# Moving the scaling, rounding and turning of attention's output rows into the next batch's attention

## The reference, cut to what matters

```
def _qdq(x):
    s = jnp.maximum(jnp.max(jnp.abs(x), axis=-1, keepdims=True) / 127.0, 1e-08)
    return jnp.clip(jnp.round(x / s), -127.0, 127.0) * s
...
attn = jax.nn.softmax(jnp.einsum('bnhd,bmhd->bhnm', q, k) * scale, axis=-1)
o = jnp.einsum('bhnm,bmhd->bnhd', attn, v).reshape(B, N, C)
out = _qdq(o) @ _qdq(wp).T + bp
...
x = x + jnp.tanh(g_xattn[1]) * _L1_xattn_ref(_layernorm(x, axis=-1), ctx_2048, ...)
x = x + jnp.tanh(g_ffn[1]) * _L1_ffn_ref(_layernorm(x, axis=-1), L1_ffn_gamma, L1_ffn_W)
return x
```

## Time and profile before

| | us |
|---|---|
| median of three runs | 973.86 |
| lowest and highest of them | 973.63, 978.19 |
| the profiled execution | 978.03 |
| its span | 976.3 |
| TensorE busy | 826.5 |
| VectorE busy | 760.4 |
| ScalarE busy | 573.4 |
| GpSimd busy | 484.2 |

### The profile page before, as it was taken

How to read it: one execution, slowest core, us unless ns; L and a number is a source line. 1 busy time by engine, 2 the same in 40 slices (tenths; PEclk the granted TensorE clock), 3 DMA queues, 4 the chain that set the end, 5 groups by cost and what they waited for, 6 DMA issues and landing times.

```text
span 976.3 us, 15239 instructions
## 1 busy us (share of the span) xinstructions
PE 826.5 (85%) x4423; PEld 359.1 (37%) x4423; DVE 760.4 (78%) x1505; ACT 573.4 (59%) x965; POOL 484.2 (50%) x560
## 2 busy tenths in 40 slices
PE   1379988778999999999999978799999999974654
PEld 1235444333444444444444433132323232222321
DVE  3958998887899998999999758477777777724884
ACT  2347888753455656556566554466666666665762
POOL 1086556322334444434444343476767666664761
PEclk9559999989999999999999995799999999996885
DMA  8536987652233323232323332312222121000111
GB/s 278 217 101 181 216 231 194 157 151 45 56 64 64 67 56 62 54 64 54 64 54 61 60 84 69 85 56 62 71 61 70 52 78 49 1 1 0 44 64 65
DMA packets 165163, 84.51 MB, mean 87 GB/s; under 512 B 116960, under 2 KB 149872, under 8 KB 165104
## 3 DMA queue, kind: packets, MB, share of 16 engines
q1 hardware_dynamic: 165104, 83.81, 34.1%
HBM read 37.50 MB, written 12.58 MB: 51 GB/s over the span
## 4 chain that ended last, share of the span: by engine, by line
PE 55%; DVE 8%; SPq 4%; issue 4%; ACT 3%; DMA 3%; POOL 0%; ACTq 0%; DVEq 0%
PE bank L1070 21%; PE bank L1082 10%; PE bank L1157 5%; PE bank L1128 5%; PE bank L1147 4%; DMA A<-B 3%; SPq L432 2%; PE bank L1273 2%; PE bank L1176 2%; PE bank L1166 2%; PE bank L1100 1%; SPq L441 1%; DVE X L1730 1%; DVE B L1611 1%; PE bank L1136 1%
## 5 line engine op out<-in xcount | busy, mean ns | idle before, releaser
L1070 PE MATMUL bank<-A,B 128*128 128x512 f16 x1024 | 232.4, 380 | 3.9 <-DVE B L1520 3.9
L1603 DVE TENSOR_REDUCE B<-bank 128x1 f32<-128x512 f32 x256 | 168.1, 683 | 73.4 <-PE bank L1128 73.3
L895 ACT ACTIVATE A<-bank 128x512 f32<-128x512 f32 x256 | 144.1, 593 | 107.0 <-PE bank L1147 103.5
L563 POOL TENSOR_TENSOR B<-B 128x512 f16<-128x512 f32 x64 | 75.5, 1180 | 209.1 <-ACT B L785 154.7
L1070 PEld LDWEIGHTS bank<-A,B 128*128 128x128 f16 x1024 | 100.2, 98 | 126.2 <-DVE B L1520 4.6
L637 POOL TENSOR_TENSOR B<-A 128x512 f32<-128x512 f32 x64 | 79.4, 1270 | 94.4 <-ACT A L895 94.4
L1082 PE MATMUL bank<-A,B 128*128 128x512 f16 x512 | 120.7, 379 | 0.0
L780 ACT ACTIVATE bank<-B 128x512 f32<-128x512 f32 x64 | 38.5, 602 | 124.6 <-DVE B L1514 124.4
L1147 PE MATMUL bank<-A 98*128 98x512 f16 x256 | 94.9, 392 | 19.5 <-ACT A L895 10.9
L1128 PE MATMUL bank<-A 96*128 96x512 f16 x256 | 98.0, 410 | 7.6 <-DMA A<-B 4.2
L637 POOL TENSOR_TENSOR B<-B,A 128x512 f32<-128x512 f32 x64 | 79.1, 1265 | 1.7 <-ACT A L895 1.7
(11 more groups left out here) (231 smaller groups left out, 1484.1 us busy)
## 6 DMA issues: line engine op xcount, KB each, us to landing
B<-in_L_ffn_w_dram SPq DMA_DIRECT2D x48, 256.0 KB, 3.8
A<-k_parts SPq DMA_DIRECT2D x48, 128.0 KB, 2.6
A<-B SPq DMA_DIRECT2D x192, 32.0 KB, 1.9
X<-in_x_dram SPq DMA_DIRECT2D x4, 1024.0 KB, 13.6
B<-in_ctx_dram SPq DMA_DIRECT2D x16, 256.0 KB, 5.2
k_parts<-B SPq DMA_DIRECT2D x16, 256.0 KB, 4.5
v_rows<-B SPq DMA_DIRECT2D x16, 256.0 KB, 2.3
B<-v_rows SPq DMA_DIRECT2D x16, 256.0 KB, 3.1
```

The costliest lines, as they stand in the source:

```text
L563: nc.gpsimd.tensor_tensor(HLb[j][:, 1, :], Db[j % 2], HLb[j][:, 0, :], ALU.subtract).then_inc(lo_done, 1)
L895: nc.scalar.activation(PR[(HG * t + j) % 8], bank[2 + j % 2][:, :], ACT.Exp, scale=SCALE).then_inc(exp_done, 1)
L1070: last = mm(bank[2 * n + q][:, :], XQT[a][:, m, :], wt[:, m % DB, j * 512:j * 512 + 512], start=(m == 0), stop=(m == 2 * DB - 1))
L1603: reduce(NMX[g % 2][:, t, j:j + 1], bank[ROW_BANKS[r % 3]][:, :], AX.X, ALU.max, negate=True).then_inc(row_max, 1)
```

## The change

For the 12 row tiles of batches 0 to 2 the preparation of the output projection moves into the attention of the next batch, one row tile per group (n = 4 to 15), with TensorE and ScalarE relieved of turning and copying them:

- VectorE, slot 11: the maximum of magnitudes of the tile (formerly at the group's end), and three small operations on its scale (formerly one set for all 12 tiles behind the last group).
- ScalarE, slot 13: scale and round the tile (formerly two tiles at a time in the last stage).
- VectorE, slot 2 of the next group: integers of the tile into `OIA`.
- SyncE, in the next group between the loads and `send_c`: a transposing DMA of 128 x 512 from `OIA` into the tile's own place in `OALL`.

In the last stage units 0 to 5 read these turned tiles directly. TensorE puts the projection of unit 0 ahead of the last two turns of attention. SyncE's loop over batches and TensorE's loop in the last stage are written out; two semaphores of the constants become one.

```diff
+        OIA = XQT[0].rearrange("p n t -> p (n t)")[:, 0:D]
...
+        AHEAD = TOK - TB
+        turned_ints = lambda i: OALL[:, i, 0:D // 2].bitcast(F16).rearrange("p (k t) -> p k t", k=DB)
...
+            def turn_o(i):
+
+                sp.wait_ge(oi_ready, i + 1)
+                sp.dma_start_transpose(turned_ints(i), OIA).then_inc(oit_in, 16)
+
             def feed(b, first, last):
                 for g in range(DB):
                     at_b, at_g = (b, DB - 1) if g == 0 else (b + 1, g - 1)
                     if not (first and g == 0 or last and g > 0):
                         load_kv(at_b, at_g, False)
                         load_q(at_b, at_g)
+                    if b * DB + g > TB:
+                        turn_o(b * DB + g - TB - 1)
                     if not (last and g == DB - 1):
                         send_c(*following(b, g))
 
-            batches(sp, feed)
+            for b in range(BATCH):
+                feed(b, b == 0, b == BATCH - 1)
+            turn_o(AHEAD - 1)
...
+                            if (t, j) == (3, 1) and not first:
+                                i = (b - 1) * TB + g
+                                act.wait_ge(osc_ready, i + 1)
+                                rows = OALL[:, bass.ds(i, 1), :].rearrange("p a d -> p (a d)")
+                                nc.scalar.activation(rows, rows, ACT.Copy, bias=RND,
+                                                     scale=OR[:, bass.ds(i, 1)]).then_inc(o_rounded, 1)
...
                 if live(s - 3):
                     pe.wait_ge(zt_out, u + 1)
                     up_to(pe, z_added, u)
-                    project(2, ZT, WLT, z_ps)
+                    project(2, half_of(ZT), WLT, z_ps)
                 if live(s):
-                    pe.wait_ge(oit_out, s + 1)
+                    if 2 * s < AHEAD:
+                        pe.wait_ge(oit_in, 16 * (2 * s + 2))
+                        src = lambda t: turned_ints(2 * s + t)
+                    else:
+                        pe.wait_ge(oit_out, s - AHEAD // 2 + 1)
+                        src = half_of(OIT)
                     up_to(pe, ro_ready, s)
-                    project(0, OIT, WPT, w_ps)
-
-            pipeline(pe, out_step)
+                    project(0, src, WPT, w_ps)
+
+            pe.wait_ge(row_max, 16 * DB * BATCH)
+            out_step(0, lambda u: 0 <= u < UNITS)
+            sum_turn(BATCH - 1, DB - 1, True)
+            o_turn(BATCH - 1, DB - 1)
+            pe.wait_ge(exp_done, 16 * DB * BATCH)
+            pe.wait_ge(den_ready, DB * BATCH)
+            pe.wait_ge(o_norm, DB * BATCH)
+            for s in range(1, UNITS + LAG):
+                out_step(s, lambda u: 0 <= u < UNITS)
...
+            def scales(n, m):
+                link(ts(OSC[:, n:m], OM[:, n:m], 1.0 / 127.0, 1e-8, ALU.mult, ALU.max))
+                link(recip(OR[:, n:m], OSC[:, n:m]))
+                ts(OST[:, n:m], OSC[:, n:m], TG[:, 1:2], None, ALU.mult).then_inc(osc_ready, 1)
+
+
+            def ints_ahead(i):
+                dve.wait_ge(o_rounded, i + 1)
+                up_to(dve, oit_in, 16 * i)
+                ts(OIA, OALL[:, i, :], RND, 127.0, ALU.subtract, ALU.min).then_inc(oi_ready, 1)
...
                             invert_sums(*preceding(b, g))
                         if slot == 9 and not opening:
                             normalize(*preceding(b, g))
+                        if slot == 2 and b * DB + g > TB:
+                            ints_ahead(b * DB + g - TB - 1)
+                        if slot == 11 and not first:
+                            i = b * DB + g - TB
+                            dve.wait_ge(o_norm, b * DB)
+                            link(reduce(OM[:, i:i + 1], OALL[:, i:i + 1, :], AX.X, ALU.max, apply_absolute_value=True))
+                            scales(i, i + 1)
                         if slot == 12 and not closing:
                             c_low(*following(b, g))
-                    if not first:
-                        if g == 0:
-                            dve.wait_ge(o_norm, b * DB)
-                        i = (b - 1) * TB + g
-                        reduce(OM[:, bass.ds(i, 1)], OALL[:, bass.ds(i, 1), :], AX.X, ALU.max, apply_absolute_value=True)
...
-            scales(0, TOK - TB)
+            ints_ahead(AHEAD - 1)
...
-                if live(s):
+                if live(s) and 2 * s >= AHEAD:
                     o_ints(s)
```

More of the change, by code:

```diff
@@ L229, in flamingo_kernel @@
         vT_ps, ctx_hi, ctx_vt, ctx_lo = sem("vT_ps"), sem("ctx_hi"), sem("ctx_vt"), sem("ctx_lo")
-        xn_ready, kT_ps, e_ready, grow_set, grow_w = sem("xn_ready"), sem("kT_ps"), sem("e_ready"), sem("grow_set"), sem("grow_w")
+        xn_ready, kT_ps, e_ready, grow_w = sem("xn_ready"), sem("kT_ps"), sem("e_ready"), sem("grow_w")
         ev_ready, ue_ready, uev_ready, scans_done = sem("ev_ready"), sem("ue_ready"), sem("uev_ready"), sem("scans_done")
@@ L260, in flamingo_kernel @@
         osc_ready, o_rounded, oi_ready, oi_ps, oit_out = sem("osc_ready"), sem("o_rounded"), sem("oi_ready"), sem("oi_ps"), sem("oit_out")
+        oit_in = sem("oit_in")
         w_ps, ro_ready, ro_scaled, x3_ready, st4, f_ready = sem("w_ps"), sem("ro_ready"), sem("ro_scaled"), sem("x3_ready"), sem("st4"), sem("f_ready")
@@ L266, in flamingo_kernel @@
         NSMALL = 9
+        CONSTS = {"ones": 3, "growth": 3 + DB, "all": 4 + DB}
         SETUP = {"vec_ps": 1, "wl_mean_ps": 2, "swp_ps": 3, "means_ps": 4}
@@ L494, in _ @@
                 nc.gpsimd.affine_select(out=GROW[:, k, :], in_=IOTA[0:DB, :], compare_op=ALU.is_equal, fill=0.0, base=-k,
-                                        pattern=[[0, SEQ]], channel_multiplier=1).then_inc(grow_set, 1)
+                                        pattern=[[0, SEQ]], channel_multiplier=1).then_inc(consts_set, 1)
             nc.gpsimd.memset(held[:, :], 0.0).then_inc(consts_set, 1)
@@ L677, in _ @@
             act.wait_ge(vec_act, 2)
-            act.wait_ge(consts_set, 4)
+            act.wait_ge(consts_set, CONSTS["all"])
             def context(n):
@@ L909, in o_round @@
             def o_round(u):
-                if u == UNITS - TB // 2:
-                    act.wait_ge(osc_ready, 2)
+                act.wait_ge(osc_ready, AHEAD + 1)
                 for t in range(2):
@@ L936, in out_step @@
                     nc.scalar.copy(ZT.rearrange("p n t -> p (n t)"), bank16[5]).then_inc(zt_out, 1)
-                if live(s):
-                    act.wait_ge(oi_ps, s + 1)
+                if live(s) and 2 * s >= AHEAD:
+                    act.wait_ge(oi_ps, s - AHEAD // 2 + 1)
                     up_to(act, w_ps, s)
                     nc.scalar.copy(OIT.rearrange("p n t -> p (n t)"), bank16[4]).then_inc(oit_out, 1)
-                if live(s + 1):
+                if live(s + 1) and 2 * (s + 1) >= AHEAD:
                     o_round(s + 1)
@@ L947, in out_step @@
                     last.then_inc(z_rounded, 1)
-            act.wait_ge(osc_ready, 1)
-            o_round(0)
             for s in range(UNITS + LAG):
@@ L956, in _ @@
             mm, turn = nc.tensor.matmul, nc.tensor.transpose
-            pe.wait_ge(consts_set, 4)
+            pe.wait_ge(consts_set, CONSTS["ones"])
             pe.wait_ge(small_in, 16 * NSMALL)
@@ L1016, in _ @@
             parts = [(p, j) for p in range(3) for j in range(DB)]
-            pe.wait_ge(grow_set, DB)
+            pe.wait_ge(consts_set, CONSTS["growth"])
             pe.wait_ge(grow_w, 1)
@@ L1255, in _ @@
             sum_weights(BATCH - 1, DB - 1)
[L1256 to L1262, removed]
             def turn_pair(to, src, done):
@@ L1272, in project @@
                     for k in range(DB):
-                        last_ = mm(bank[first_bank + t][:, :], src[:, DB * t + k, :], wt[:, k, :],
+                        last_ = mm(bank[first_bank + t][:, :], src(t)[:, k, :], wt[:, k, :],
                                    start=(k == 0), stop=(k == DB - 1))
                 last_.then_inc(done, 1)
+            half_of = lambda both: lambda t: both[:, DB * t:DB * t + DB, :]
             def out_step(s, live):
@@ L1282, in out_step @@
                     turn_pair(bank16[5], ZI, zi_ps)
-                if live(s):
-                    pe.wait_ge(oi_ready, s + 1)
-                    up_to(pe, oit_out, s)
+                if live(s) and 2 * s >= AHEAD:
+                    pe.wait_ge(oi_ready, s + AHEAD // 2 + 1)
+                    up_to(pe, oit_out, s - AHEAD // 2)
                     turn_pair(bank16[4], OI, oi_ps)
@@ L1358, in _ @@
             ts(ints[2], wl_raw, 1.0, None, ALU.min).then_inc(ints_done, 1)
-            dve.wait_ge(consts_set, 4)
+            dve.wait_ge(consts_set, CONSTS["all"])
             diag = T32[:, 2, :].rearrange("p (k r) -> p k r", k=DB)
@@ L1688, in o_ints @@
             def o_ints(u):
-                dve.wait_ge(o_rounded, u + 1)
-                up_to(dve, oi_ps, u)
+                dve.wait_ge(o_rounded, u + AHEAD // 2 + 1)
```

(1 more changed line is left out.)

## The result

| | before | changed |
|---|---|---|
| median, 20 runs each | 976.64 | 978.12 |
| lowest to highest | 972.53 to 978.91 | 974.79 to 982.28 |
| profiled execution's span | 976.3 | 974.3 |

The ratio changed to before is 1.0025, with a 95% interval of 1.0013 to 1.0037: 2.4 us slower on 976.6, which is less than the 0.5% that counts as a change here. The interval, 1.3 to 3.6 us, leaves out zero, but it is far too wide to confirm a tenth; the two medians differ by 1.5. The forecast was +2.4, and 0.2 for the clock.

The account below looks back on a forecast made before the run. In attention the offset chain from `c_low`, not TensorE's own work, bounds each group; the last stage's head waits for its pipeline to fill. -10.3 + 12.7 = +2.4 on 973.86 gives 976.3, plus 0.2: 976.5 us, range 965 to 982.

Parts of the forecast that it names:

- 0.2 for the clock: Last stage: small allowance for TensorE's clock, raising the forecast from 976.3 to 976.5 us.
- The chain sets the group's end, and VectorE has no slack ahead of it: Attention: the offset chain from `c_low` to TensorE, 3.28 us, ends each group; VectorE reaches `c_low` back to back.
- Loss 10 x 1.27 = 12.7: Attention, groups 4 to 13: slot 11's reduction (0.67) and three small operations (0.60) delay `c_low` 1.27 us each.
- Gain at the head, 10.3: Head of last stage: unit 0's projection directly behind the sums' matmuls brings the first `z_stats` 10.3 us earlier.
- The sign of 9 us: Last stage's head: a first `z_stats` later than 9 us behind the sums would show the prediction wrong.
- No gain in the steps behind it: Last stage, units 0 to 5: dropped `o_ints`, turns, copy and roundings gain nothing; `z_scales` starts when it did.
- Hidden parts: Attention: slot 2 integers (about 0.35 us), slot 13 rounding (0.72) and the transposing DMA fit in existing gaps.
- Attention loses its clock: Rival: longer TensorE waits send attention to half clock in every third group, +10 us, 986; chance 0.08.
- The transposing DMA in `send_c`'s way: Rival: SyncE's DMA issue slips 1.9 us, delaying the chain in groups 5 to 13, +11.4, 987.7 us; chance 0.16.
- Hidden work: Rival: work added in attention is hidden, loss at most 0.4 us per group, result 963.6 to 967.6; chance 0.16.

Follow-up runs that it names:

- the block moved away: Changed kernel with slot 11's maximum of magnitudes and three scale operations put behind `c_low` in slot 12: 967.33 us, ratio 0.9909 to the kernel before.
- the block alone: Kernel before with only the slot 11 reduction and three small scale operations added, their old counterparts removed: 988.86 us, ratio 1.014 to the kernel before.
- the doubled reduction: Changed kernel with the reduction of slot 11 done twice, output unchanged: 995.29 us, ratio 1.0179 to the kernel before.
- the three versions with the scale work behind `c_low`: Changed kernel with scale work in slot 12: 967.33 us; also rounding in the next group's slot 1: 967.68; also `c_out` and `c_low` earlier: 962.13.
- the late projection: Changed kernel with unit 0's projection back behind attention's last turns and the waits for the last normalize: 982.56 us, ratio 1.0067 to the kernel before.

## Why the prediction was right, step by step

- *The chain sets the group's end, and VectorE has no slack ahead of it*: right, and shown from both sides, by the block moved away (0.9909) and by the block alone (1.014).
- *Loss 10 x 1.27 = 12.7*: the ten groups are right, the size was 0.2 too large. It measured 1.05: `c_low` came 1.13 later (0.71 from the reduction's start to the next operation's, not 0.67; 0.51 for the three small operations on one column, not 0.60; and the two maxima, now apart, take 0.09 less together), less some 0.06 behind it, in the issue of `send_c` (1.29 instead of 1.34). SyncE's list is written out in the changed kernel; in the run with the block alone it is in a loop as before, and the wait there is 1.53 instead of 1.47. Ten groups make 10.4 us.
- *Gain at the head, 10.3*: 10.0. The projection ran at full clock and L941 came 2.9 us behind the start of the sums, as forecast. VectorE was not free in time, though: its scale operation L1653 took 2.18 us instead of 0.17, and `z_stats` began 0.4 us behind GpSimd's result. The sign of 9 us held if counted from the end of the sums, 8.6, as the forecast's own sum does.
- *No gain in the steps behind it*: the last stage took 82.5 us before and 81.9 after. In the other executions it took 81.1 to 84.1 without the 48 turns, and 82.7 with them. The waits of `z_scales` took up what `o_ints` left; in a step of the same kind their wait is 0.86 us where it was 0.26, as forecast:

```profile
912.93 1.29 DVE L1743 TENSOR_TENSOR B<-bank,gam_all 128x512 f32<-128x512 f32 x2 [0.86 <-ACT bank L950]
```

  An effect of the clock there cannot be told from the variation between executions, 3 us.
- *Hidden parts*: the integers took 0.42 in their gap, the rounding 0.71 in its own, the DMA was hidden (1.0025 without it).
- *Attention loses its clock*: held at 0.08 and as all or nothing. It happened in part: one stretch of 3.4 us at half clock in the profiled execution, 1.6 us; and with the doubled reduction some 8 of the 15 us by which that run was slower. A loss counted 2.3 too large and a clock hardly counted offset each other: by the trace the sum is -10.0 + 10.4 + 1.6 = +2.0, with a last stage taken as unchanged, against +2.4 measured, which is itself known only to within 1.2 us. The hit to the tenth is luck; the two large terms are not.
- *The transposing DMA in `send_c`'s way*, 0.16: too much for 2 us of room; it had 2.45. *Hidden work*, 0.16: refuted.

## What to carry to other kernels

Idle time of an engine says nothing on where an operation may stand. Find the once-per-period chain that the bottleneck waits for, and put new work on its engines behind their link in it: the same four instructions, two places further down, were worth 11 us. Where the bottleneck engine's wait grows, count more than the wait itself, and see in the windows whether its clock held.

## What was not expected of the hardware

TensorE's granted clock in attention depended on the length of one wait per group. With waits of 0.4 to 0.9 us no stretch at half clock lay between the starts of groups 2 and 15 in any of the four kernels profiled (before, and the three versions with the scale work behind `c_low`). With waits near 1.45 (one of 2.19 among them, with none behind it) three of four profiled executions had one of 3.4 us and one had none. With waits of 2.05 to 2.2 there were six, 23.9 us in all; with the waits filled by matmuls whose result is thrown away, none. All nine stretches began between 0.4 us before and 1.6 us behind the end of such a wait. These are single executions, but the mean clocks of all timed ones agree: 0.922 to 0.937 with the doubled reduction, 0.937 to 0.946 with its wait filled. The Trainium skill (TensorE: Matmul & The Clock Gate, HAM oscillation) describes such a fall behind waits for DMAs between short stretches of matmuls. This trace agrees on the waits; the stretches between them were not short here, TensorE being busy for 178.78 of 208.30 us.

A VectorE operation of 128x4 that takes 0.17 us with GpSimd idle (889.28, the late projection) took 2.18 beside GpSimd's L671, and both ended together: 889.80 + 2.18 = 891.98 and 889.62 + 2.34 = 891.96. The integers of 128x512 took 0.42 in slot 2 with GpSimd idle (748.25), and 1.50 at 879.82 beside its additions, of which one had started at 879.78 and ended at 881.03. The Trainium skill (SBUF — State Buffer, Who interferes with whom) has a rule for this: a VectorE operation that runs in a 2-port mode, as `tensor_scalar` can, needs a pair of ports that it shares with GpSimd, and whoever comes second is blocked for the other's whole operation. The two pairs above fit it; no run was made to separate it from another cause.
